# Masked queries on GpSimd and a later output projection in the second attention of a language-model tower

## The chip, the cores and the metric

The kernel runs on one NeuronCore of a Trainium2 chip as a single program. The metric is the device time of one execution in microseconds (us); lower is better. Within the core five engines run their own instruction streams and meet only at semaphores: TensorE (PE, matrix products into the eight PSUM banks; PEld is its weight load), VectorE (DVE), ScalarE (ACT), GpSimd (POOL) and SyncE (SP, transfers).

## The reference, cut to what matters

A tower of layers works on 16 sequences of 128 tokens: a token model (embedding, memory, four MLP layers, head), a fast-weight attention, a mixture of experts, then a second attention, then a second mixture of experts. The part that the change touches is the second attention (64 channels, 8 heads of 8):

```python
qk = (x @ Wqk.T).reshape(Bb, Nn, 2, Hh, hd)
patch_score = softmax(einsum('bhnd,bhmd->bhnm', q, k) * scale)
pos_score = softmax((rel @ Wpos.T + bpos).transpose(2, 0, 1))
g = sigmoid(gating)[None, :, None, None]
attn = (1.0 - g) * patch_score + g * pos_score[None]
attn = attn / attn.sum(axis=-1, keepdims=True)
out = einsum('bhnm,bhmd->bhnd', attn, v).transpose(0, 2, 1, 3).reshape(Bb, Nn, Cc)
return out @ Wproj.T + bproj
```

It is fed with the layer norm of the residual stream h, and its result is added to h; the last mixture of experts normalises that sum again.

## The kernel before, in words

All data is float32. The 16 sequences are the tiles t = 0 to 15 of 128 tokens each, and four of them make a chunk c (CH = 4, NC = 4). The residual stream stays in SBUF as H. Every engine's order is written out by hand: each block of the program is a list of calls to small helpers, and what an engine waits for is written as semaphore waits.

The second attention is a loop over the 16 tiles ("step t", j = t mod 4) on TensorE, ScalarE and VectorE, each with its own loop body. One step does, per engine:

- TensorE: scores(t+1) (8 products into banks 2 and 3, L1768 and L1769), on every odd step values_back (L1805, into bank 7), values(t-1) (L1792, bank 6), and turn_scores(t) (eight transposes of the exponentiated scores into banks 4 and 5, L1780). Once per chunk, spread over its four steps, it also does work for the next chunk: turn_input (L1815, bank 0) at j = 0, project_qk (L1824 and L1825: queries to bank 1, keys to bank 0) at j = 1, project_v (L1830, bank 1) at j = 3. positional (L1839, bank 1) comes at steps 4 and 12. At steps 7, 11 and 15 it turns the attended tiles of the chunk before (turn_attended, L1849, bank 0) and after turn_scores multiplies them with the output weights (project_out, L1855, bank 0).
- VectorE: normalise(t): for each of the two score banks a maximum (L2493) and a subtraction into SBUF (L2497). scores(t+1) can only start when this is done, since there is one pair of score banks; normalise(t+1) can only start when scores(t+1) is done. Then come, per chunk, the work around the norms: mix (reciprocal of the sums, gate, two more operations, L2507 to L2514, at j = 2; two of the four read two tensors of SBUF, L2509 and L2514), add_attended (L2520, adds project_out's bank to H) with e_stats (L409, L412) at j = 0, and e_apply (four TENSOR_SCALAR of L424) at j = 1.
- ScalarE: take_turned(t-1) (L1225, two copies of banks 4 and 5 to SBUF), the exponential of step t (L1242), save_values_T (L1217) on even steps, and per chunk: take_x (L1184), queries (L1189), take_keys (L1194), take_values (L1198), take_attended (L1203), take_positions (L1209).

The heads are separated by masks. A chunk's queries are copied four times out of bank 1, each time scaled by another column of the mask m4 (one scale per partition), into the four planes of qd[c % 2]: queries(c, h0, h1), L1189. For chunks 1 to 3 two of the four copies are made at step 4(c-1)+1 and two at the step after it. The first scores of a chunk wait for all four (semaphore d_qd), and so does project_v, since it overwrites bank 1.

GpSimd has little to do here: the norms' reciprocal roots (rstd_twice, L400 and L402) and some adds.

## Time and profile before

| | |
|---|---|
| median of 3 runs | 621.32 us |
| runs | 621.87, 620.23, 621.32 us |
| the profiled execution | 620.74 us |
| its span, first to last instruction | 619.0 us |
| mean granted TensorE clock | 0.984 |
| busy: PE, DVE, ACT, POOL | 545.0, 427.1, 358.0, 347.0 us |
| second attention (scores of tile 0 to the last turn_scores) | about 478 to 553 us |

Starts are microseconds from the span's first instruction. The profiled execution's own time is 1.7 us more than its span and 0.6 us below the median. In the timeline a row is one instruction, or several equal ones in a row merged (xN); a bracket at its end is the idle time of its engine just before it and what ended it.

### The profile page before, as it was taken

Reading aid. Unit: us, or ns where it says so; the run is one execution under the profiler, and the core shown is the slowest. Engines: PE = TensorE matmul, PEld = TensorE weight load, DVE = VectorE, ACT = ScalarE, POOL = GpSimd, SP = SyncE. Lnnn points to the kernel's source line nnn. Section 1 sums busy time; section 2 is a strip of 40 time slices with the busy share of each in tenths; the row PEclk is TensorE's granted clock in tenths of the full one; section 3 lists DMA queues with packets and bytes.
Section 4 is the critical chain, followed back from the end, with each engine's and each line's share of the span. In section 5 each row is a group of like instructions: output and inputs, shape, how many; then the busy total and the mean of one; then the engine's idle time right before and its main releaser. Section 6 shows DMA issues by size and latency. Waiting matters only on the chain.

```text
span 619.0 us, 12438 instructions
## 1 busy us (share of the span) xinstructions
PE 545.0 (88%) x4494; PEld 414.5 (67%) x4494; DVE 427.1 (69%) x1088; ACT 358.0 (58%) x949; POOL 347.0 (56%) x474
## 2 busy tenths in 40 slices
PE   7989999999987867779788888998999698889996
PEld 3556767778434656558677777886578576765785
DVE  4943563423887868798989988899526987756444
ACT  1264444444676765224768878874696666757430
POOL 2597653311360767798889899998267310001445
PEclk9999999999999999987999999999999999989999
DMA  8000000000000434300000000000000000000000
GB/s 278 17 1 1 2 0 1 1 1 1 1 2 1 75 71 77 81 0 2 2 1 1 1 2 2 0 2 1 2 2 2 1 2 1 2 2 1 9 9 18
DMA packets 10860, 10.43 MB, mean 17 GB/s; under 512 B 6000, under 2 KB 9840, under 8 KB 10544
## 3 DMA queue, kind: packets, MB, share of 16 engines
q1 hardware_dynamic: 8080, 7.54, 4.5%
q0 software_dynamic: 2144, 1.75, 1.5%
q8 instruction: 36, 0.59, 0.4%
q10 hardware_dynamic: 576, 0.35, 0.2%
q14 instruction: 24, 0.20, 0.1%
HBM read 5.77 MB, written 0.52 MB: 10 GB/s over the span
## 4 chain that ended last, share of the span: by engine, by line
PE 52%; DVE 21%; POOL 9%; ACT 7%; issue 5%; DMA 4%; SPq 2%; DVEq 0%; POOLq 0%; ACTq 0%
PE bank L1354 8%; PE bank L1342 7%; PE bank L1441 7%; PE bank L1657 5%; PE bank L1723 5%; DVE bank L2173 3%; PE bank L1615 3%; DVE features L2167 2%; DMA coefs<-weights 2%; PE bank L1720 2%; PE bank L1432 2%; POOL features L600 2%; PE bank L1768 2%; DVE features L2143 2%; SPq L460 2%
## 5 line engine op out<-in xcount | busy, mean ns | idle before, releaser
L1441 PE MATMUL bank<-ident,features 128*128 128x128 f32 x604 | 79.0, 280 | 10.4 <-DVE features L2143 7.1
L1441 PEld LDWEIGHTS bank<-ident,features 128*128 128x128 f32 x604 | 69.0, 145 | 19.0 <-DVE features L2143 13.8
L909 ACT ACTIVATE G<-bank,cols 128x512 f32<-128x512 f32 x64 | 43.9, 687 | 52.9 <-PE bank L1342 52.9
L600 POOL TENSOR_TENSOR features<-UV,coefs 128x1024 f32<-128x1024 f32 (+3 forms) x36 | 59.8, 1684 | 4.0 <-DVE UV L2130 4.0
L1354 PE MATMUL bank<-weights,G 128*128 128x128 f32 x512 | 59.9, 275 | 0.0
L1342 PE MATMUL bank<-xs,weights 128*128 128x512 f32 x128 | 57.8, 594 | 0.9 <-ACT xs L900 0.9
L1354 PEld LDWEIGHTS bank<-weights,G 128*128 128x128 f32 x512 | 58.5, 192 | 0.0
L2143 DVE TENSOR_TENSOR features<-UV,bank 128x1024 f32<-128x1024 f32 (+3 forms) x68 | 55.6, 861 | 0.7 <-ACT bank L992 0.2
L400 POOL TENSOR_SCALAR rstd<-mv 128x4 f32<-128x4 f32 x8 | 1.6, 195 | 92.7 <-DVE mv L412 92.7
L999 ACT ACTIVATE xs<-UV,coefs 128x32 f32<-128x32 f32 x232 | 50.4, 308 | 0.0
L999 ACT ACTIVATE sx<-UV,coefs 128x32 f32<-128x32 f32 x200 | 43.5, 307 | 0.0
L573 POOL TENSOR_TENSOR UV<-xs,rows 128x512 f32<-128x512 f32 x16 | 20.2, 1270 | 38.7 <-DVE xs L2032 38.6
L1432 PE MATMUL bank<-features 32*128 32x136 f32 x768 | 32.4, 299 | 10.4 <-issue 2.8
L2173 DVE TENSOR_REDUCE bank<-features 128x32 f32<-128x1024 f32 (+3 forms) x40 | 41.0, 1050 | 0.0
L1342 PEld LDWEIGHTS bank<-xs,weights 128*128 128x128 f32 x128 | 23.1, 190 | 25.0 <-issue 22.7
L1615 PE MATMUL bank<-RK,ident 128*128 128x256 f32 x160 | 38.3, 388 | 0.0
L424 DVE TENSOR_SCALAR UV<-xs,mv,rstd 128x128 f32<-128x128 f32 x52 | 20.8, 462 | 24.9 <-POOL rstd L393 23.2
L1432 PEld LDWEIGHTS bank<-features 32*128 32x128 f32 x768 | 27.0, 193 | 15.9 <-issue 5.5
L393 POOL TENSOR_TENSOR rstd<-rstd,neghalf 128x4 f32<-128x4 f32 x32 | 33.4, 1045 | 2.7
L2032 DVE TENSOR_TENSOR xs<-bank,UV 128x512 f32<-128x512 f32 x16 | 11.0, 690 | 33.2 <-PE bank L1354 31.2
L2167 DVE TENSOR_TENSOR features<-RK,bank 128x1024 f32<-128x1024 f32 (+3 forms) x32 | 32.2, 1007 | 0.8
L1615 PEld LDWEIGHTS bank<-RK,ident 128*128 128x128 f32 x160 | 29.7, 194 | 3.5
(362 smaller groups left out, 1348.0 us busy)
## 6 DMA issues: line engine op xcount, KB each, us to landing
weights<-in_w SPq DMA_DIRECT2D x2, 1024.0 KB, 10.2
features<-in_tok SPq DMA_DIRECT2D x1, 768.0 KB, 5.8
weights<-in_ew SPq DMA_DIRECT2D x4, 128.0 KB, 3.1
weights<-in_ew SPq DMA_DIRECT2D x2, 256.0 KB, 2.9
coefs<-G POOLq DMA_DIRECT2D x16, 25.5 KB, 4.7
rows<-in_rows SPq DMA_DIRECT2D x1, 384.0 KB, 6.4
out_h<-H SPq DMA_DIRECT2D x3, 128.0 KB, 2.0
coefs<-G SPq DMA_DIRECT2D x14, 25.5 KB, 5.1
```

Source lines behind the costliest of these rows:

```text
L393: pool.tensor_tensor(rstd[:, k, 0:n], rstd[:, k, 0:n], neghalf[:, 0:n], ALU.pow).then_inc(s["ln_rstd"], 1)
L600: pool.tensor_tensor(out, u, co, ALU.mult).then_inc(s["held_p"], 1)
L909: act.activation(G[:, 4 * (w % 2) + f, :], up_bank(f)[:], ACT.Gelu, bias=col("b1", 4 * i + f)).then_inc(s["tok_gelu"], 1)
L999: last = act.activation(own[t % 2][:, k, DH * h:DH * h + DH], UV[:, FIRST[t] + k, 0, DH * h:DH * h + DH], ACT.Copy, scale=C[:, t, 2 * NH + ...
L1342: mm(up_bank(f)[:], w1[:, i, P * f:P * f + P], xT[:, w % 2, :], start=True, stop=True).then_inc(s["tok_up"], 1)
L1354: last = mm(down_bank(w)[:, DT * j:DT * j + DT], G[:, 4 * (w % 2) + f, P * j:P * j + P], w2[:, i, f, :], start=(f == 0), stop=(f == 3))
L1432: last = mm(bank[4 * k + j][:, GB * SL * n:GB * SL * n + GB * SL], feat[left + k][x, g, 0:T].rearrange("p s b -> p (s b)"), feat[right + k ...
L1441: last = mm(out[:, P * k:P * k + P], x[:, P * k:P * k + P], ident[:], is_transpose=True, start=first and k == 0, stop=last_ and k == n - 1 ...
L1615: mm(bank[1][:, HB:2 * HB], ident[:], RK[:, 0, :], start=True, stop=True)
L2143: dve.tensor_tensor(out, u, co.unsqueeze(3).broadcast_to([P, R, NH, DH]), ALU.mult)\
L2167: ch(dve.tensor_tensor(PD[:, j, 0:R * HB].rearrange("p (r x) -> p r x", r=R), RK[:, r0:r1_, :], e.unsqueeze(1).broadcast_to([P, R, HB]), A ...
L2173: ch(dve.tensor_reduce(bankCR[:, r0:r1_, :], PD[:, j, 0:(r1_ - r0) * HB].rearrange("p (r h j) -> p r h j", r=r1_ - r0, h=NH), AX_X, ALU.add))
```

## The change

Six things differ.

1. ScalarE makes no masked queries for chunks 2 and 3. At step 5 and step 9 it makes one plain copy of bank 1 into a free buffer of SBUF (take_queries, target qraw), in the place of two scaled copies; the two of steps 6 and 10 go. Chunks 0 and 1 stay as they were.
2. GpSimd makes these four planes from qraw with four TENSOR_SCALAR multiplications of 128x512 per chunk, chunk 2 before and chunk 3 after the root of the norm of chunk 0's result.
3. project_v of chunks 2 and 3 waits for the plain copy alone; the first scores of chunks 2 and 3 wait for GpSimd (d_qpool).
4. project_out of chunks 0 and 1 moves on TensorE from the end of steps 7 and 11 to the end of steps 8 and 12, and writes bank 1, not bank 0. For that bank it also waits for take_values of chunk c+2 and, for chunk 1, for take_positions. turn_input(3) no longer waits for the addition but for take_attended(0); project_qk(3) now waits for the addition.
5. On VectorE add_attended and e_stats move from steps 8 and 12 to steps 9 and 13; e_apply moves from steps 9 and 13 to step 11 and step 14 (there behind mix).
6. Two semaphores are merged into others (utab_mm into u_mm, mean_mm into router_mm) with the counts of the later waits raised by one. Nothing is added or taken from the instructions there.

```diff
+        qraw = FT[:, 8704:9216]
...
+        def out_bank(c):
+
+            return bank[1 if c < 2 else 0]
...
             rstd_pool(pool, ch, ("d", NC - 1), CH)
             second_norm(NC - 1)
-            for c in range(NC):
+            def queries(c):
+
+                pool.wait_ge(s["q_raw"], c - 1)
+                for h in range(NH // 2):
+                    pool.tensor_scalar(qd[c % 2][:, h, :], qraw, m4[:, h:h + 1], None, ALU.mult).then_inc(s["d_qpool"], 1)
+
+            queries(2)
+            rstd_twice(pool, ch, ("e", 0), CH)
+            queries(3)
+            for c in range(1, NC):
                 rstd_twice(pool, ch, ("e", c), CH)
...
+            def take_queries(c):
+
+                act.wait_ge(s["d_q"], c + 1)
+                if c == 3:
+                    act.wait_ge(s["d_qpool"], NH // 2)
+                act.activation(qraw, bank[1][:], ACT.Copy).then_inc(s["q_raw"], 1)
...
                     elif j == 1:
-                        queries(c + 1, 0, 2)
+                        if c:
+                            take_queries(c + 1)
+                        else:
+                            queries(1, 0, 2)
                         take_keys(c + 1)
                     elif j == 2:
-                        queries(c + 1, 2, NH // 2)
+                        if not c:
+                            queries(1, 2, NH // 2)
...
                 if t % CH == 0:
-                    pe.wait_ge(s["d_qd"], NH // 2 * (t // CH + 1))
+                    if t < 2 * CH:
+                        pe.wait_ge(s["d_qd"], NH // 2 * (t // CH + 1))
+                    else:
+                        pe.wait_ge(s["d_qpool"], NH // 2 * (t // CH - 1))
...
             def project_out(c):
                 pe.wait_ge(s["at_xT"], c + 1)
+                if c < 2:
+                    pe.wait_ge(s["d_vcopy"], c + 3)
+                if c == 1:
+                    pe.wait_ge(s["pos_saved"], 2)
                 for j in range(CH):
-                    last = mm(bank[0][:, D * j:D * j + D], xa[:, 1, P * j:P * j + P], wproj[:], start=True, stop=True)
+                    last = mm(out_bank(c)[:, D * j:D * j + D], xa[:, 1, P * j:P * j + P], wproj[:], start=True, stop=True)
...
-                if j == 3 and c:
-                    project_out(c - 1)
+                if t == T - 1 or j == 0 and c >= 2:
+                    project_out(NC - 2 if j else c - 2)
...
-                if j == 0 and c >= 2:
+                if j == 1 and c >= 2:
                     add_attended(c - 2)
                     e_stats(c - 2)
-                if j == 1 and c >= 2:
-                    e_apply(c - 2)
                 if j == 2 and c:
                     mix(c - 1)
+                if t in (11, 14):
+                    e_apply(c - 2)
```

TensorE at the end of step 7, before (L1849 turn_attended(0), L1830 project_v(2), L1780 turn_scores(7), L1855 project_out(0), L1768 the first product of scores(9)):

```order
L1849 MATMUL bank0<-ident,RK 64x128 [waits d_kcopy,comb_done]
L1830 MATMUL bank1<-weights,sx 128x64 [waits d_qd]
L1780 MATMUL bank4<-ident,features 128x128 [waits p_ready,s_exp]
L1780 MATMUL bank5<-ident,features 128x128 [waits p_ready]
L1855 MATMUL bank0<-weights,sx 128x64 [waits at_xT]
L1768 MATMUL bank2<-features 128x128 [waits s_sub]
```

The same place now, and on to the first product of scores(10) (new lines: L1882 turn_attended, L1863 project_v, L1808 turn_scores, L1796 scores, L1820 values, L1843 turn_input, L1892 project_out; rows in between are the rest of the same groups):

```order
L1882 MATMUL bank0<-ident,RK 64x128 [waits d_kcopy,comb_done]
L1863 MATMUL bank1<-weights,sx 128x64 [waits q_raw]
L1808 MATMUL bank4<-ident,features 128x128 [waits p_ready,s_exp]
L1796 MATMUL bank2<-features 128x128 [waits s_sub]
L1820 MATMUL bank6<-UV,coefs 32x128 [waits p_ready]
L1843 MATMUL bank0<-ident,UV 128x128 [waits at_xT,d_kcopy,d_norm]
L1892 MATMUL bank1<-weights,sx 128x64 [waits d_vcopy,at_xT]
L1796 MATMUL bank2<-features 128x128 [waits s_sub]
```

project_out(0) now stands behind turn_scores(8), one pair of scores later, and writes bank 1.

VectorE in steps 13 and 14, before (L424 e_apply(1), L2493 and L2497 normalise(14), L2507 to L2514 mix(2)):

```order
L424 TENSOR_SCALAR xs<-H,mv,rstd 128x128 [waits ln_rstd,ln_var]
L424 TENSOR_SCALAR xs<-H,mv,rstd 128x128 x3
L2493 TENSOR_REDUCE RK<-bank2 128x4 [waits s_mm0]
L2497 TENSOR_TENSOR features<-bank2,RK 128x512 [waits dve_chain,s_T]
L2493 TENSOR_REDUCE RK<-bank3 128x4 [waits s_mm1]
L2497 TENSOR_TENSOR features<-bank3,RK 128x512 [waits dve_chain]
L2507 RECIPROCAL comb<-bank7 128x32 [waits at_T,pos_saved,av_back]
L2509 TENSOR_TENSOR comb<-comb,gate 128x32 [waits dve_chain]
L2512 TENSOR_TENSOR RK<-bank7,comb 128x256 [waits dve_chain]
L2514 TENSOR_TENSOR RK<-RK 128x256 [waits dve_chain]
L2493 TENSOR_REDUCE RK<-bank2 128x4 [waits s_mm0]
```

The same place now, from the end of normalise(14) to the start of normalise(15) (L429 is e_apply(1), L2544 to L2551 mix(2)):

```order
L2544 RECIPROCAL comb<-bank7 128x32 [waits at_T,pos_saved,av_back]
L2546 TENSOR_TENSOR comb<-comb,gate 128x32 [waits dve_chain]
L2549 TENSOR_TENSOR RK<-bank7,comb 128x256 [waits dve_chain]
L2551 TENSOR_TENSOR RK<-RK 128x256 [waits dve_chain]
L429 TENSOR_SCALAR xs<-H,mv,rstd 128x128 [waits ln_rstd,ln_var]
L429 TENSOR_SCALAR xs<-H,mv,rstd 128x128 x3
L2530 TENSOR_REDUCE RK<-bank2 128x4 [waits s_mm0]
```

e_apply(1) has moved from ahead of normalise(14) to between mix(2) and normalise(15); in its old place stand the addition and e_stats of chunk 1.

GpSimd behind the last add of the norms (L843), now (L879 the queries, L405 and L407 the root of chunk 0's norm):

```order
L843 TENSOR_TENSOR H<-H,rows 128x256 [waits d_norm]
L879 TENSOR_SCALAR features<-features,m4 128x512 [waits q_raw]
L879 TENSOR_SCALAR features<-features,m4 128x512 x3
L405 TENSOR_SCALAR rstd<-mv 128x4 [waits ln_var]
L407 TENSOR_TENSOR rstd<-rstd,neghalf 128x4 [waits pool_chain]
L879 TENSOR_SCALAR coefs<-features,m4 128x512 [waits q_raw]
L879 TENSOR_SCALAR coefs<-features,m4 128x512 x3
```

Before, the roots followed directly on the add.

## Rows read from the trace of the kernel before

**Rows 1.** The page: shares of the chain that ended last, by engine.

```profile
PE 52%; DVE 21%; POOL 9%; ACT 7%; issue 5%; DMA 4%; SPq 2%; DVEq 0%; POOLq 0%; ACTq 0%
```

**Rows 2.** Timeline of DVE, steps 6 to 10: start us, us, what [idle before].

```profile
509.49 0.69 DVE L2493 TENSOR_REDUCE RK<-bank 128x4 f32<-128x512 f32 x1
...
511.61 0.69 DVE L2497 TENSOR_TENSOR features<-bank,RK 128x512 f32<-128x512 f32 x1
513.94 0.69 DVE L2493 TENSOR_REDUCE RK<-bank 128x4 f32<-128x512 f32 x1 [1.64 <-PE bank L1768]
...
518.22 0.42 DVE L2520 TENSOR_TENSOR H<-bank,H 128x256 f32<-128x256 f32 x1 [1.48 <-PE bank L1855]
...
519.62 0.66 DVE L2493 TENSOR_REDUCE RK<-bank 128x4 f32<-128x512 f32 x1
...
523.64 0.69 DVE L2493 TENSOR_REDUCE RK<-bank 128x4 f32<-128x512 f32 x1 [0.23 <-PE bank L1768]
```

**Rows 3.** Timeline of PE, from scores(8) to scores(9), and turn_scores(8).

```profile
512.74 0.37 PE L1768 MATMUL bank<-features 64*128 64x128 f32 x1 [0.55 <-ACT features L1189]
...
516.30 1.04 PE L1780 MATMUL bank<-ident,features 128*128 128x128 f32 x8
517.18 1.00 PE L1855 MATMUL bank<-weights,sx 128*128 128x64 f32 x8
518.12 0.37 PE L1768 MATMUL bank<-features 64*128 64x128 f32 x1
...
520.27 1.04 PE L1780 MATMUL bank<-ident,features 128*128 128x128 f32 x8
```

**Rows 4.** Timeline of ACT, step 5: the first two masked queries of chunk 2.

```profile
507.37 1.27 ACT L1189 ACTIVATE features<-bank,m 128x512 f32<-128x512 f32 x2 [1.62 <-PE bank L1824]
```

**Rows 5.** Timeline of PE: the first products of scores(12), scores(13) and scores(14).

```profile
531.23 0.37 PE L1768 MATMUL bank<-coefs 64*128 64x128 f32 x1 [0.55 <-ACT coefs L1189]
...
536.60 0.37 PE L1768 MATMUL bank<-coefs 64*128 64x128 f32 x1
...
541.08 0.37 PE L1768 MATMUL bank<-coefs 64*128 64x128 f32 x1
```

**Rows 6.** Timeline of DVE: starts of normalise(13), e_apply(1), normalise(14), normalise(15).

```profile
538.11 0.66 DVE L2493 TENSOR_REDUCE RK<-bank 128x4 f32<-128x512 f32 x1
...
540.80 1.11 DVE L424 TENSOR_SCALAR xs<-H,mv,rstd 128x128 f32<-128x128 f32 x4
542.27 0.69 DVE L2493 TENSOR_REDUCE RK<-bank 128x4 f32<-128x512 f32 x1 [0.36 <-PE bank L1768]
...
546.40 0.69 DVE L2493 TENSOR_REDUCE RK<-bank 128x4 f32<-128x512 f32 x1
```

**Rows 7.** Timelines of ACT and of PE at step 15, the attention's end.

```profile
549.87 0.59 ACT L1203 ACTIVATE sx<-bank 64x512 f32<-64x512 f32 x1 [1.29 <-PE bank L1849]
550.36 1.04 ACT L1242 ACTIVATE features<-features 128x1024 f32<-128x1024 f32 x1
...
551.46 1.57 PE L1780 MATMUL bank<-ident,features 128*128 128x128 f32 x8 [1.63 <-ACT features L1242]
```

**Rows 8.** Stretches: us, busy (x) of PE, PEld, DVE, ACT, POOL, then PEclk, DMA, GB/s.

```profile
551.50:555.50 4.00, 4.00 (x22) 4.00 (x23) 0.80 (x4) 1.20 (x2) 0.00 (x0) 0.57 0.00 0
```

**Rows 9.** GpSimd operations of 128x512, grouped by form: xcount | busy us, mean ns.

```profile
L800 POOL COPY xs<-sx 128x512 f32<-128x512 f32 x2 | 1.2, 610 | 0.1
L573 POOL TENSOR_TENSOR UV<-xs,rows 128x512 f32<-128x512 f32 x16 | 20.2, 1270 | 38.7 <-DVE xs L2032 38.6
L450 POOL TENSOR_TENSOR coefs<-coefs 128x512 f32<-128x512 f32 x1 | 1.5, 1514 | 0.1
```

**Rows 10.** Timelines of DVE and POOL: L2380 without and with GpSimd beside it.

```profile
564.19 0.68 DVE L2380 TENSOR_TENSOR coefs<-RK 128x512 f32<-128x512 f32 x1
584.21 0.94 DVE L2380 TENSOR_TENSOR coefs<-RK 128x512 f32<-128x512 f32 x1
...
584.68 0.78 POOL L880 TENSOR_TENSOR H<-H,features 128x128 f32<-128x128 f32 x1
```

More of the change, by code:

```diff
@@ L1295, in _ @@
             pe.wait_ge(s["load_tables"], 32)
-            mm(bank[0][0:VOC, 0:DT], embT[:], wupd[:], start=True, stop=True).then_inc(s["utab_mm"], 1)
+            mm(bank[0][0:VOC, 0:DT], embT[:], wupd[:], start=True, stop=True).then_inc(s["u_mm"], 1)
             pe.wait_ge(s["tables_ready"], 1)
@@ L1623, in means @@
                 if c == NC - 1:
-                    last.then_inc(s["mean_mm"], 1)
+                    last.then_inc(s["router_mm"], 1)
             tr = nc.tensor.transpose
@@ L1812, in turn_input @@
                 if c >= 3:
-                    pe.wait_ge(s["d_add"], c - 2)
+                    pe.wait_ge(s["at_xT"], c - 2)
                 for j in range(CH):
@@ L1823, in project_qk @@
                     pe.wait_ge(s["pos_saved"], 1)
+                if c >= 3:
+                    pe.wait_ge(s["d_add"], c - 2)
                 mm(bank[1][:], wq, xa[0:D, 0, :], start=True, stop=True).then_inc(s["d_q"], 1)
@@ L1827, in project_v @@
             def project_v(c):
-                pe.wait_ge(s["d_qd"], NH // 2 * (c + 1))
+                if c < 2:
+                    pe.wait_ge(s["d_qd"], NH // 2 * (c + 1))
+                else:
+                    pe.wait_ge(s["q_raw"], c - 1)
                 for j in range(CH):
@@ L1978, in _ @@
             one_hot(1)
-            dve.wait_ge(s["utab_mm"], 1)
+            dve.wait_ge(s["u_mm"], 1)
             dve.wait_ge(s["load_update"], 16)
@@ L1993, in memory @@
             def memory(c):
-                dve.wait_ge(s["u_mm"], c + 1)
+                dve.wait_ge(s["u_mm"], c + 2)
                 dve.tensor_tensor_scan(memT[:, 512 * c:512 * c + 512], keep[:, 512 * c:512 * c + 512],
@@ L2416, in _ @@
             CAPACITY = float(-(-N * 5 // (4 * E)))
-            dve.wait_ge(s["router_mm"], 1)
+            dve.wait_ge(s["router_mm"], 2)
             ch(tt(rout[0:T, 3, :], bank[7][0:T, 64:64 + E], row("br0", parts=T), plus))
@@ L2420, in _ @@
             small_softmax(rout[0:T, 3, :], 0, rout[0:T, 0, :]).then_inc(s["r_prob"], 1)
-            dve.wait_ge(s["router_mm"], 2)
+            dve.wait_ge(s["router_mm"], 3)
             sc = rout[0:T, 4, :]
```

13 lines of the change are left out of this document (7 added, 6 removed).

## The prediction

> **What bounds the kernel now.** I read the chain of waits first: TensorE and VectorE hold 73% of it [rows 1], and in the second attention they hand it to each other once per step, with two detours over ScalarE. So I read that stage in the timelines of the engines. scores(t+1) needs normalise(t) done; normalise(t+1) needs scores(t+1). From the first row of normalise(7) at 509.49 to the end of its last at 511.61 + 0.69 = 512.30 are 2.80 us, and from the first product of scores(8) to normalise(8) are 513.94 - 512.74 = 1.20 us [rows 2, 3]. That makes 4.0 us a step if nothing else is in the way; normalise(9) to normalise(10) has it, 523.64 - 519.62 = 4.02 [rows 2]. Two steps are far above it: normalise(8) to normalise(9) takes 519.62 - 513.94 = 5.68, and its twin, a chunk later, ends at 538.11 [rows 2, 6]. In both TensorE is the late one, and project_out is the last thing in its queue ahead of the scores: it starts at 517.18, the scores at 518.12 [rows 3], while normalise(8) was over at 516.74 (513.94 + 2.80). The reader should also see two waits on ScalarE: scores(8) and scores(12) each follow 0.55 us of idle TensorE, ended by the last masked query [rows 3, 5].
>
> **The change, part by part.** I follow the start of normalise(t) and call its shift against the profile d(t).
>
> Queries of chunk 2. normalise(7) ends at 512.30, so without the query wait scores(8) could start at 512.36 and not at 512.74: d(8) = -0.38 [rows 2, 3]. This needs GpSimd done by 512.3. The plain copy can start where the first masked one did, 507.37 [rows 4]; two masked ones took 1.27 together, so one copy takes about 0.6 and GpSimd starts at 508.05. It has 4.3 us for four operations, **1.07 us each**. The trace shows no multiplication of this kind on GpSimd. Nearest rows of 128x512: a copy 0.61 us, a product of two tensors 1.27 and once 1.51 [rows 9]. The new operation reads one tensor, as the copy does, and computes, as the product does; I take 0.8, nearer to the copy, and keep 0.61 and 1.51 as ends. At 0.8 it is done at 511.3 and hidden. For chunk 3 the same working gives a start of about 525.05 and scores(12) at 529.45, 4.4 us, 1.1 each.
>
> The Trainium skill, "GPSIMD Engine Reference", section "Performance versus the Vector engine", gives about 1.8 cycles per element as the best for a tight one-operation loop and says that elementwise work belongs on VectorE; an estimate from it is 0.77 us for 512 elements, which would leave the sum as it is. No run here shows it yet.
>
> project_out(0) out of step 7. From scores(8) to project_out are 517.18 - 512.74 = 4.44 us of TensorE work (values_back, values, turn_attended, project_v, turn_scores) [rows 3]. scores(9) now stands in its place: about 512.36 + 4.44 + 0.1 = 516.9 (the 0.1 because a group of scores behind transposes starts that much later), and normalise(9) 1.2 later, at 518.1, with no addition ahead of it: d(9) = 518.1 - 519.62 = -1.5.
>
> project_out(0) into step 8. From scores(9) to turn_scores(8) are 520.27 - 518.12 = 2.15 us, and eight transposes hold the queue for 517.18 - 516.30 = 0.88: 3.0 us, and 4.0 with the projection's 0.94 (518.12 - 517.18) [rows 3], so scores(10) can start at 516.9 + 4.0 = 520.9. normalise(9) ends at 518.1 + 2.8 = 520.9: the projection fits. Behind it VectorE now does the addition and e_stats, 519.62 - 518.22 = 1.40 us [rows 2], 521.0 to 522.4, where scores(10) is done at 522.1: d(10) = 522.4 - 523.64 = -1.2. Step 10 goes on as before with mix(1) as its limit, d(11) about -1.35.
>
> Step 11. Without the query wait scores(12) starts at the end of normalise(11), 529.45, against 531.23 [rows 5]; e_apply(0), 1.11 us [rows 6], is over at 530.4, before scores(12) is: d(12) = -1.8. TensorE's queue to scores(13) was 536.60 - 531.23 = 5.37 [rows 5], now 0.94 less: scores(13) at 533.9, normalise(13) at 535.1, **d(13) = -3.0**.
>
> Then most of the second half is paid back. Step 12 holds positional, and its queue was already full: 541.08 - 536.60 = 4.48 [rows 5]. With project_out(1) it is 5.4, so scores(14) starts at 539.3. VectorE waits for that projection for its addition, and with e_stats (1.40) normalise(14) begins at 540.75: d(14) = -1.5. Behind normalise(14) now stand mix(2) (1.4, from the end of the four rows to 546.40, rows 6) and e_apply(1), which was hidden in step 13: 540.75 + 2.7 + 1.4 + 1.1 = 546.0, against 546.40. d(15) is only -0.4.
>
> The end. normalise(15) ends at 546.0 + 2.8 = 548.8, but what counts is the exponential of step 15, which started at 550.36, not at VectorE's end (549.20): take_attended(2) at 549.87 stood ahead of it in ScalarE's queue [rows 7]. That path follows scores(15), which needs normalise(14). From the start of normalise(14) to that exponential were 550.36 - 542.27 = 8.1 us [rows 6, 7], so it comes at 540.75 + 8.1 = 548.85. Both meet there: **-1.5 us** at the last turn_scores. Behind it the same program runs with TensorE busy to the end, so the shift is passed on whole. ScalarE's saved copies count no further: it idles in every step.
>
> GpSimd against VectorE. The new operations run from 508.05 and 525.05, just when mix(0) (it lies right ahead of 509.49, rows 2) and mix(1) stand on VectorE ahead of a normalise that waits for them. L2380, which reads two tensors of SBUF, took 0.68 us alone and 0.94 with a GpSimd operation beside it, itself 0.78 long [rows 10]. mix has two operations with two SBUF inputs. I take 0.2 us for each mix, 0.4 in sum; bounds 0 and 4 x 0.26 = 1.0. Both delays pass on, since TensorE's queue follows.
>
> The semaphore merges raise counts that are passed in the same order: nothing, or below what can be measured. Sum: -1.5 + 0.4 = **-1.1 us**, 620.74 - 1.1 = 619.6 for a profiled execution and 621.32 - 1.1 = **620.2** for the median (the profiled one lay 0.6 below it).
>
> **The rivals.** A measurement of this kernel tells about 0.3% (1.9 us) from no change.
>
> A: the forecast, -1.1, from -1.9 to 0 with the bounds of the contention and of the GpSimd price up to 1.27. Chance 0.58.
>
> B: GpSimd locks VectorE out. If each two-input operation of mix waits for a whole GpSimd operation, half of 0.8 on average and at worst all of it, four of them cost 1.6 to 3.2 instead of 0.4: +0.1 to +1.7, time about 621.6. For it: the 0.26 of rows 10. Against: that is a third of the GpSimd operation, not the whole. The Trainium skill, "SBUF — State Buffer", section "Who interferes with whom", says that the shared port pair is an exclusive lock held for the whole instruction, and that a VectorE instruction with two SBUF inputs contends with a GpSimd one that reads SBUF. By that rule the case is this rival; rows 10 agree in direction, not in size. Chance 0.12.
>
> C: slower, by GpSimd's price. Above 1.07 us every 0.1 costs 0.4 at scores(8) and, above 1.1, as much at scores(12). At 1.27 it is 0.8 + 0.7 = 1.5: the gain is gone. From there on the kernel is slower; at 1.51 [rows 9] it is (1.51 - 1.07) x 4 + (1.51 - 1.10) x 4 = 3.4, less 1.5: +1.9, 623.2. For it: one row of a simple product had 1.51. Against: that one reads two tensors. Chance 0.10.
>
> D: more than forecast, by the clock. At the attention's end TensorE idled 1.63 us before turn_scores(15) [rows 7], and in the 4 us after it the granted clock is 0.57, at its lower level of 1.2 GHz for most of them: 4 x 0.43 = 1.7 us lost [rows 8]. In my schedule both ends of that idle time move by 1.5 us (the one follows scores(15), the other VectorE), so it stays about as long and I expect the fall to stay. If it went, the change would give -2.8, 618.5. Chance 0.20, in which smaller slips of mine in step 13 to 15, where the 3.0 us of d(13) shrink to 1.5, are counted too.
>
> **How the numbers follow.** 620.2 is the likeliest. The range runs from 618.5 (D) to 622.6 (B at its worst with half of the 0.6 by which medians stray here); what lies outside is the dear end of C and a deeper fall of the clock, under 0.2. Faster by over 0.3% (below 619.5): D and the edge of A, 0.25. Slower by over 0.3% (above 623.2): the dear part of C, with 0.04 for a longer low clock, 0.10. The rest, 0.65, is within.
>
> **What the profile of the changed kernel would show.** GpSimd's multiplications at about 0.8 us, the last of four done before the idle time of scores(8) ends; scores(8) and scores(12) released by normalise, not by queries. normalise(8) to normalise(9) near 4.5 us instead of 5.68. A gap on VectorE ahead of the addition of chunk 1, and over 5 us from normalise(14) to normalise(15), with mix and e_apply in it. The last turn_scores about 1 us earlier. The forecast is wrong if a multiplication takes over 1.1 us, if mix grows by more than 0.5 us, or if the stretch at the lower clock behind step 15 changes its length.

## The result

| | median us | runs | lowest to highest |
|---|---|---|---|
| kernel before | 619.70 | 8 | 617.82 to 621.87 |
| changed kernel | 625.64 | 8 | 624.18 to 628.74 |

The ratio is 1.010, with a 95% interval of 1.0071 to 1.013: the change makes the kernel slower, by 5.9 us between the medians. The forecast was 1.1 us faster, and its range ended at 622.6. The profiled execution of the changed kernel took 624.18 us, with a span of 622.3 (before: 620.74 and 619.0). Here and below medians are over all executions of a kernel, while ratios leave out the few that took over 1.5% longer than the kernel's fastest (the traces of e1 and e2 are of such executions).

GpSimd's timeline is the first thing to read: start us, us, what, xcount, idle time before and its releaser. The four masked queries of chunk 2 and of chunk 3, and one operation by itself:

```profile
507.45 6.21 POOL L879 TENSOR_SCALAR features<-features,m 128x512 f32<-128x512 f32 x4 [3.28 <-ACT features L1211]
509.01 1.57 POOL L879 TENSOR_SCALAR features<-features,m 128x512 f32<-128x512 f32 x1
527.91 6.31 POOL L879 TENSOR_SCALAR coefs<-features,m 128x512 f32<-128x512 f32 x4 [1.21 <-ACT features L1211]
```

One operation takes 1.56 to 1.58 us by itself and 1.55 in a row of four, not 0.8 (one of the eight, which runs beside VectorE's e_apply, takes 1.68). Its source came when the prediction said: all of this trace lies 0.63 us earlier, from stages that the change doesn't touch, and 507.45 + 0.63 = 508.08, where the prediction had 508.05. So the four end at 513.66, which is 514.29 on the prediction's time axis, where it had 511.3: 3.0 us later. TensorE's timeline shows who waits for that (L1808 turn_scores, L1796 scores, L1833 values_back, L1820 values, L1892 project_out):

```profile
509.81 1.09 PE L1808 MATMUL bank<-ident,features 128*128 128x128 f32 x8 [0.30 <-ACT features L1263]
513.71 0.37 PE L1796 MATMUL bank<-features 64*128 64x128 f32 x1 [2.81 <-POOL features L879]
...
515.21 1.11 PE L1833 MATMUL bank<-picked,UV 128*128 128x128 f32 x4
516.25 1.08 PE L1820 MATMUL bank<-UV,coefs 128*32 128x128 f32 x16
...
518.77 1.04 PE L1808 MATMUL bank<-ident,features 128*128 128x128 f32 x8
519.75 0.37 PE L1796 MATMUL bank<-features 64*128 64x128 f32 x1
...
520.84 0.64 PE L1820 MATMUL bank<-UV,coefs 128*32 128x128 f32 x16
...
522.78 1.00 PE L1892 MATMUL bank<-weights,sx 128*128 128x64 f32 x8
523.80 0.37 PE L1796 MATMUL bank<-features 64*128 64x128 f32 x1
```

Where [rows 3] had 0.55 us of idle time ahead of scores(8), there are 2.81 now, ended by GpSimd. A second thing stands in these rows: the 16 instructions of values take 1.08 us right after the wait and 0.64 a step later. The granted clock tells why. TensorE alone, in four stretches of the changed kernel: us, busy (x), PEclk, DMA share, GB/s.

```profile
510.00:515.00 5.00, 2.19 (x24) 0.93 0.00 0
515.00:516.00 1.00, 1.00 (x8) 0.50 0.00 0
515.00:520.00 5.00, 5.00 (x48) 0.73 0.01 3
535.00:540.00 5.00, 5.00 (x49) 0.68 0.00 0
```

From about 0.6 us behind each of the two waits, TensorE is granted 0.50, its lower level of 1.2 GHz, for some 3 us, though it is then busy without a gap. Before the change the clock was 1.00 in all these steps.

VectorE's timeline of the changed kernel has the counterpart of [rows 2] and [rows 6] (L2530 opens a normalise, L2546 and L2551 are the operations of mix with two SBUF inputs, L2557 the addition, L429 e_apply):

```profile
507.64 0.54 DVE L2546 TENSOR_TENSOR comb<-comb,gate 128x32 f32<-128x32 f32 x1
...
508.67 0.42 DVE L2551 TENSOR_TENSOR RK<-RK 128x256 f32<-128x256 f32 x1
...
515.30 0.69 DVE L2530 TENSOR_REDUCE RK<-bank 128x4 f32<-128x512 f32 x1 [3.48 <-PE bank L1796]
...
520.94 0.69 DVE L2530 TENSOR_REDUCE RK<-bank 128x4 f32<-128x512 f32 x1 [2.83 <-PE bank L1796]
...
528.29 0.35 DVE L2546 TENSOR_TENSOR comb<-comb,gate 128x32 f32<-128x32 f32 x1
...
532.20 1.48 DVE L429 TENSOR_SCALAR xs<-H,mv,rstd 128x128 f32<-128x128 f32 x4
...
545.86 0.42 DVE L2557 TENSOR_TENSOR H<-bank,H 128x256 f32<-128x256 f32 x1 [1.55 <-PE bank L1892]
...
551.36 1.11 DVE L429 TENSOR_SCALAR xs<-H,mv,rstd 128x128 f32<-128x128 f32 x4
```

From such rows I took the start of every normalise and lined up the steps of all kernels at normalise(0). This table carries most of what follows. A column gives the us from one normalise to the next, the last row the whole stage from normalise(0) to the exponential of step 15. "Forecast" is the prediction's schedule written in the same way, without its 0.4 for contention. The last three columns are experiments told of below.

| step | before | forecast | changed | e1 | e3 | e12 |
|---|---|---|---|---|---|---|
| 0 to 7 | 30.06 | 30.06 | 30.21 | 30.07 | 30.88 | 30.23 |
| 7 to 8 | 4.45 | 4.07 | **6.29** | 4.44 | 4.10 | 5.88 |
| 8 to 9 | 5.68 | 4.56 | **5.64** | 4.53 | 4.57 | 4.54 |
| 9 to 10 | 4.02 | 4.32 | 4.28 | 4.28 | 4.27 | 4.27 |
| 10 to 11 | 4.33 | 4.18 | 4.26 | 4.11 | 4.92 | 4.26 |
| 11 to 12 | 4.45 | 4.00 | **6.46** | 4.45 | 4.11 | 5.99 |
| 12 to 13 | 5.69 | 4.49 | **5.56** | 4.52 | 4.56 | 4.53 |
| 13 to 14 | 4.16 | 5.66 | 5.76 | 5.77 | 5.76 | 5.76 |
| 14 to 15 | 4.13 | 5.23 | 5.13 | 5.12 | 5.12 | 5.13 |
| 15 to exponential | 3.96 | 2.86 | 2.93 | 2.93 | 2.94 | 2.93 |
| stage | 70.93 | 69.43 | 76.52 | 70.22 | 71.23 | 73.52 |

The changed kernel's stage is 5.59 us longer than before, and the medians differ by 5.9. Against the forecast four steps are off, two per wait for GpSimd; the other steps agree to 0.15 us.

At the attention's end the fall of the clock [rows 8] isn't in this trace, although TensorE idles for the same time before turn_scores(15). The first row is TensorE's timeline of the changed kernel:

```profile
556.41 1.09 PE L1808 MATMUL bank<-ident,features 128*128 128x128 f32 x8 [1.63 <-ACT features L1263]
```

The second is the stretch behind it:

```profile
556.40:560.40 4.00, 3.99 (x43) 1.00 0.00 0
```

### The profile page after: what moved, and what is told of

Same layout as the page of the kernel before. It is cut to its first block, busy times and chain, and to the rows that moved or that the text cites. A ratio compares the mean times of both kernels' runs of the same rounds, so it can differ in the third digit from the quotient of the medians.

```text
span 622.3 us, 12444 instructions
## 1 busy us (share of the span) xinstructions
PE 544.4 (87%) x4494; PEld 413.9 (67%) x4494; DVE 427.9 (69%) x1088; ACT 354.8 (57%) x943; POOL 359.7 (58%) x482
## 3 DMA queue, kind: packets, MB, share of 16 engines
HBM read 5.77 MB, written 0.52 MB: 10 GB/s over the span
## 4 chain that ended last, share of the span: by engine, by line
PE 33%; DVE 15%; POOL 7%; ACT 4%; issue 2%; DVEq 0%; POOLq 0%
PE bank L1466 6%; PE bank L1682 5%; PE bank L1748 5%; DVE bank L2210 3%; PE bank L1640 2%; DVE features L2204 2%; PE bank L1745 2%; PE bank L1796 2%; POOL features L605 2%; DVE features L2180 2%; PE bank L1820 1%; PE bank L1808 1%; POOL features L625 1%; POOL coefs L879 1%; DVE features L2534 1%
## 5 line engine op out<-in xcount | busy, mean ns | idle before, releaser
L1466 PE MATMUL bank<-ident,features 128*128 128x128 f32 x604 | 76.1, 275 | 11.3 <-DVE features L2180 8.2
L1466 PEld LDWEIGHTS bank<-ident,features 128*128 128x128 f32 x604 | 66.8, 142 | 18.8 <-DVE features L2180 14.1
L405 POOL TENSOR_SCALAR rstd<-mv 128x4 f32<-128x4 f32 x8 | 1.6, 195 | 79.5 <-DVE mv L417 79.5
L1457 PE MATMUL bank<-features 32*128 32x136 f32 x768 | 34.0, 307 | 11.6 <-issue 4.2
L1457 PEld LDWEIGHTS bank<-features 32*128 32x128 f32 x768 | 28.4, 199 | 17.2 <-issue 7.6
L429 DVE TENSOR_SCALAR UV<-xs,mv,rstd 128x128 f32<-128x128 f32 x52 | 20.8, 463 | 24.9 <-POOL rstd L398 23.2
```

Source lines behind the costliest of these rows:

```text
L1457: last = mm(bank[4 * k + j][:, GB * SL * n:GB * SL * n + GB * SL], feat[left + k][x, g, 0:T].rearrange("p s b -> p (s b)"), feat[right + k ...
L1466: last = mm(out[:, P * k:P * k + P], x[:, P * k:P * k + P], ident[:], is_transpose=True, start=first and k == 0, stop=last_ and k == n - 1 ...
```

## The experiments

The theory after the first reading: (1) a GpSimd multiplication costs 1.55 us, which makes scores(8) and scores(12) wait; (2) that idle time brings the clock down, which costs as much again; (3) the moved projection works as forecast. Rivals: the moved projection itself delays a step and the query wait only fills what it leaves; the slow steps 8 to 9 and 12 to 13 come from contention or from bank 1; GpSimd holds VectorE up. In the diffs, a line with + is the experiment's. Each ratio is to the kernel before, timed beside the experiment; a time without a ratio is of one execution.

### One part alone: e1 and e2

e1 keeps the moved projection, and ScalarE makes all masked queries as before (the waits that belong to them are as before too).

```diff
-            queries(2)
-            rstd_twice(pool, ch, ("e", 0), CH)
-            queries(3)
-            for c in range(1, NC):
+            for c in range(NC):
...
-                        if c:
-                            take_queries(c + 1)
-                        else:
-                            queries(1, 0, 2)
+                        queries(c + 1, 0, 2)
```

> The changed kernel with ScalarE making all masked queries again, as in the kernel before; the later output projection, its bank and the moved norm steps stay. Theory (the loss is GpSimd's: its masked multiplication took 1.55 us instead of the forecast 0.8, so scores(8) and scores(12) wait for it, and TensorE's clock falls in those waits): without it 1.1 to 1.5 us below the kernel before, no fall of the clock behind scores(8) and scores(12), normalise(8) to normalise(9) near 4.5 us. Rival (the moved projection and norm steps cost by themselves, in steps 12 to 14): at or above the kernel before, by 1 us or more.

e2 keeps GpSimd's queries and puts project_out (with its bank and its waits), the addition, e_stats and e_apply back to where they were.

```diff
-                if t == T - 1 or j == 0 and c >= 2:
-                    project_out(NC - 2 if j else c - 2)
+                if j == 3 and c:
+                    project_out(c - 1)
```

> The kernel before with the masked queries of chunks 2 and 3 on GpSimd and nothing else of the change. Theory (GpSimd's price): the start of scores(8) 1.4 to 1.9 us later than before and that of scores(12) 3 to 4, plus about 1 us for each fall of the clock behind them: 4 to 7 us above the kernel before, like the changed kernel or above it. Rival (the moved projection is what costs): within 1.5 us of the kernel before.

e1: 619.25 us, ratio 0.9973 (0.9943 to 1.0003), stage 70.22. e2: 629.2 us, ratio 1.0128 (1.0093 to 1.0163), stage 78.25. So the queries alone cost more than the whole change, somewhat above the 4 to 7 us expected, and the projection alone is worth 0.7 us in the stage (1.1 to 1.5 were expected; as a time it is 1.7, with an interval that just reaches the kernel before). The parts don't simply add: 7.3 - 0.7 = 6.6, and the whole change has 5.6. The missing 1.0 us lies between normalise(11) and normalise(13): 14.16 us in e2 against 10.14 before, 12.02 in the changed kernel against 8.97 in e1. There e2's clock is low for over 6 us, twice as long as in the changed kernel; what sets that length isn't shown. VectorE's timeline of e1 shows the prediction's d(9) as forecast, 525.66 - 521.13 = 4.53, and so its twin, 543.02 - 538.50 = 4.52, with the gap ahead of the addition of chunk 1 (L2544):

```profile
521.13 0.69 DVE L2517 TENSOR_REDUCE RK<-bank 128x4 f32<-128x512 f32 x1 [1.63 <-PE bank L1786]
...
525.66 0.69 DVE L2517 TENSOR_REDUCE RK<-bank 128x4 f32<-128x512 f32 x1 [1.72 <-PE bank L1786]
...
533.01 0.19 DVE L2533 TENSOR_TENSOR comb<-comb,gate 128x32 f32<-128x32 f32 x1
...
538.50 0.69 DVE L2517 TENSOR_REDUCE RK<-bank 128x4 f32<-128x512 f32 x1 [0.61 <-PE bank L1786]
...
543.02 0.69 DVE L2517 TENSOR_REDUCE RK<-bank 128x4 f32<-128x512 f32 x1 [1.72 <-PE bank L1786]
...
547.39 0.42 DVE L2544 TENSOR_TENSOR H<-bank,H 128x256 f32<-128x256 f32 x1 [1.55 <-PE bank L1879]
```

The rivals that blame the projection or bank 1 fall with that. In e2 TensorE's clock falls in the same two places:

```profile
515.00:520.00 5.00, 3.71 (x36) 0.66 0.00 0
...
537.00:543.00 6.00, 5.12 (x42) 0.50 0.00 0
```

### The price of GpSimd's operation: e3 and e4

e3 makes the same planes with a TENSOR_TENSOR, the mask's column repeated along the row as the second input.

```diff
-                    pool.tensor_scalar(qd[c % 2][:, h, :], qraw, m4[:, h:h + 1], None, ALU.mult).then_inc(s["d_qpool"], 1)
+                    pool.tensor_tensor(qd[c % 2][:, h, :], qraw, m4[:, h:h + 1].broadcast_to([P, CH * P]), ALU.mult)\
+                        .then_inc(s["d_qpool"], 1)
```

> The changed kernel with GpSimd multiplying by the mask column as a second tensor read over and over (step 0) in a tensor-tensor product, not as a scalar per partition. Theory (only the duration of this operation decides): it takes 1.04 to 1.27 us as the other products of 128x512 do; then scores(8) is late by at most 0.8 us against 2.0 now, and the total is 3 to 6 us below the changed kernel, between -1.5 and +1 against the kernel before. Rival (any GpSimd work in that place delays VectorE and TensorE, whatever it takes): 2 us or less below the changed kernel.

e4 leaves the masks of chunks 2 and 3 out and copies qraw four times.

```diff
-                    pool.tensor_scalar(qd[c % 2][:, h, :], qraw, m4[:, h:h + 1], None, ALU.mult).then_inc(s["d_qpool"], 1)
+                    pool.tensor_copy(qd[c % 2][:, h, :], qraw).then_inc(s["d_qpool"], 1)
```

> The changed kernel with GpSimd copying the raw queries into the four planes instead of multiplying them with the mask; the masks of chunks 2 and 3 are left out, so this part of the output is not computed as the reference does. Theory (the duration of one GpSimd operation is the cause): at the copy's 0.61 us the four are done in 2.5, scores(8) and scores(12) are released by VectorE or TensorE, the clock stays up behind them, and the stage from normalise(0) to the last exponential is 69.5 to 70.0 us, against 70.9 before and 76.5 in the changed kernel. Rival (a GpSimd beside VectorE is enough of a cost): mix(0) and mix(1) stretched so far that the stage stays above 70.9.

e3: 621.52 us, ratio 1.0021 (0.9991 to 1.0052), stage 71.23. e4: 620.66 us in a single execution, stage 70.53, above the 69.5 to 70.0 that was expected. GpSimd's timeline of e3, the four of chunk 2 and two by themselves:

```profile
508.80 4.21 POOL L879 TENSOR_TENSOR features<-features,m 128x512 f32<-128x512 f32 x4 [3.25 <-ACT features L1212]
508.80 1.04 POOL L879 TENSOR_TENSOR features<-features,m 128x512 f32<-128x512 f32 x1 [3.25 <-ACT features L1212]
509.80 1.04 POOL L879 TENSOR_TENSOR features<-features,m 128x512 f32<-128x512 f32 x1
```

The product takes 1.04 us where the same work as TENSOR_SCALAR takes 1.57, and the copy of e4 takes 0.61. At 1.04 both waits are gone: 7 to 8 takes 4.10, 11 to 12 takes 4.11, no clock falls, and 8 to 9 and 12 to 13 are 4.57 and 4.56. Every step is then as forecast but those that hold a mix: 0 to 7 is 0.82 longer than before, 10 to 11 is 0.74 longer than forecast. VectorE's timeline of e3 at mix(0):

```profile
509.02 0.87 DVE L2547 TENSOR_TENSOR comb<-comb,gate 128x32 f32<-128x32 f32 x1
509.92 0.42 DVE L2550 TENSOR_TENSOR RK<-bank,comb 128x256 f32<-128x256 f32 x1
510.38 0.74 DVE L2552 TENSOR_TENSOR RK<-RK 128x256 f32<-128x256 f32 x1
```

L2550, with one input in PSUM, keeps its length. L2547 takes 0.87 where e1 has 0.19 at the same place of mix(1), and it ends at 509.89, 0.05 after the GpSimd operation that ran at its start (508.80 + 1.04 = 509.84). L2552 takes 0.74, not 0.42, and ends at 511.12, 0.28 after the one that ran at its start (509.80 + 1.04 = 510.84). At mix(1) it is the same, 0.68 and 0.74. In e4, with copies of 0.61 beside them, the two take 0.43 and 0.85 at mix(0) and 0.24 and 0.85 at mix(1). In all eight cases the shorter operation ends 0.04 or 0.05 us, the longer one 0.28 or 0.29 us after the end of the GpSimd operation that had begun last before it. So the wait is that for the rest of a GpSimd operation, as rival B had it: 1.56 us in e3 for both mixes together. That is a reading of eight operations in two kernels.

The Trainium skill, "SBUF — State Buffer", section "Who interferes with whom", has the shared port pair as an exclusive lock for the whole instruction; these rows agree with that rule. Those with GpSimd's TENSOR_SCALAR don't, which reads one tensor and one scalar per partition: in the changed kernel L2546 (507.64 + 0.54) ends at 508.18, in the middle of a GpSimd operation that runs from 507.45 to 509.03, and L2551 keeps its 0.42. There the wait has another end: L2546 ends 0.73 us after the start of the GpSimd operation at mix(0), and 0.73 after it at mix(1) (528.64 against 527.91), though it began at 0.19 in the one and at 0.38 in the other. The same operation in e2, e5, e5b and e12 has 0.72 to 0.74; that makes ten cases in five kernels. So GpSimd's TENSOR_SCALAR held it up for the first part of its 1.57 us only; why is open.

### The clock in the two waits: e5, e5b and e12

These keep the changed kernel whole and give TensorE dummy products while it waits for GpSimd. They write a part of bank 1 that nobody reads any more.

```diff
+                if t in (2 * CH, 3 * CH):
+                    pe.wait_ge(s["q_raw"], t // CH - 1)
+                    for k in range(26):
+                        mm(bank[1][:, 256:384], ident[:], ident[:], start=True, stop=True)
```

> The changed kernel with 26 products of the identity with itself (128x128, result unused, into bank 1) on TensorE ahead of scores(8) and of scores(12), so that the engine works through most of the wait for GpSimd. Theory that the fall of the clock in these waits is a part of the loss: granted clock 1.0 behind both, normalise(8) to normalise(9) about 4.5 us instead of 5.64, and 2.0 to 2.5 us below the changed kernel in the stage. Rival (the long steps 8 and 12 come from the order of the work, not from the clock): no change from the changed kernel.

26 products were too many: they last longer than the wait, and normalise(7) to normalise(8) takes 8.82 us, 2.5 more than in the changed kernel. The time is 626.53 (ratio 1.0109, 1.0063 to 1.0155), so as a time it settles nothing, and the 2.0 to 2.5 us that the stage was to gain are missed. The step behind the wait does settle it: 4.53 us and not 5.64, in an otherwise equal program. So e5b has 12 of them, and e12 is the same kernel as e5b, timed ten times.

```diff
-                    for k in range(26):
+                    for k in range(12):
```

> As the filler experiment before, with 12 products instead of 26: those took 5.5 us and kept scores(8) waiting themselves, 12 take about 2.6 and end before GpSimd does. Theory (each fall of the clock costs 1.1 us): normalise(8) at the same place as in the changed kernel (36.5 us after normalise(0)), then 4.5 us to normalise(9) instead of 5.64, and a stage of 74.3 us instead of 76.5. Rival: the stage stays at 76.5.

> The changed kernel with 12 dummy products of 128x128 in each of the two waits for GpSimd (the kernel of e5b again, now timed in rounds): TensorE is kept at work through part of the wait, nothing is spared. One execution of e5b had 618.66 with a stage of 73.52 us against 76.52 in the changed kernel. If the fall of the clock in the two waits is what that difference is, it holds here: about 3 us below the changed kernel, ratio to before 1.005 or less. If e5b's one time was chance, the ratio is that of the changed kernel, 1.010.

e5b: 618.66 in a single execution, stage 73.52. e12: 623.36 us, ratio 1.004 (1.0009 to 1.0071), stage 73.52 again. Both stages are 0.8 below the 74.3 that was expected, since the scores right behind the wait run at the full clock too. The single 618.66 was a lucky one as a time, but the stage was not: e12's profiled execution took 626.64 with the same stage, and from 222 to 306 us, in stages that no experiment touches, the granted clock was 0.96 in e5b's and 0.88 in e12's. TensorE's timeline of e12, the wait for GpSimd filled and the scores behind it:

```profile
516.21 2.84 PE L1790 MATMUL bank<-ident 128*128 128x128 f32 x24
519.18 0.37 PE L1800 MATMUL bank<-features 64*128 64x128 f32 x1
...
520.27 0.66 PE L1837 MATMUL bank<-picked,UV 128*128 128x128 f32 x4
520.86 0.64 PE L1824 MATMUL bank<-UV,coefs 128*32 128x128 f32 x16
```

And TensorE alone in two stretches of e12 that hold both waits and what follows:

```profile
517.00:522.00 5.00, 4.87 (x61) 1.00 0.01 3
537.00:542.00 5.00, 4.78 (x60) 1.00 0.01 3
```

scores(8) still waits for GpSimd's fourth multiplication (512.92 + 6.20 = 519.12 in e12), and nothing else is spared; the work only keeps the clock at its higher level of 2.4 GHz. That is worth (6.29 - 5.88) + (5.64 - 4.54) = 1.5 us at chunk 2 and (6.46 - 5.99) + (5.56 - 4.53) = 1.5 us at chunk 3: **3.0 us of the changed kernel's loss are clock**, shown by adding work. As times the two kernels differ by 1.010 - 1.004 = 0.006 of 620, 3.7 us. Nor is the fall there a matter of one trace: it stands behind all four waits for GpSimd that TensorE spent idle (2.78 to 2.90 us, in the changed kernel and e2) and behind none of the six that were filled (e5, e5b, e12).

### Further with the projection: e7 and e9

With the queries on ScalarE, their wait can be shortened in place. e7 is e1 with the second two masked queries of chunks 2 and 3 behind the exponential of steps 6 and 10, and e_apply(1) at step 15, behind normalise(15).

```diff
+                if j == 2 and 0 < c < 3:
+                    queries(c + 1, 2, NH // 2)
                 if t and t % 2 == 0:
                     save_values_T(t // 2 - 1)
...
-                if t in (11, 14):
+                if t in (11, 15):
                     e_apply(c - 2)
```

> The later projection without GpSimd's queries, with two more edits: at steps 6 and 10 ScalarE makes the last two masked queries ahead of save_values_T, not behind it, and VectorE does e_apply of chunk 1 behind normalise(15), not ahead of it. If the two waits for the last query (0.55 us each) come only from that place in ScalarE's queue, and the payback in step 14 only from e_apply, the stage falls from 70.2 to 68.4 us, and the kernel lies 2.5 us below the one before (4 with the fall of the clock at the attention's end gone). If ScalarE's or TensorE's queue is the limit there, 69.5 or more.

e9 is e7 with project_out(1) at step 13 and its addition and e_stats at step 15; the wait of turn_attended for the addition stays for the last chunk alone.

```diff
-                if t == T - 1 or j == 0 and c >= 2:
-                    project_out(NC - 2 if j else c - 2)
+                if t in (8, 13, 15):
+                    project_out((8, 13, 15).index(t))
...
-                if j == 1 and c >= 2:
+                if t in (9, 15):
                     add_attended(c - 2)
                     e_stats(c - 2)
```

> As the kernel with the two edits, and the projection of chunk 1 one step later still, at step 13, where TensorE has no positional work; its addition and norm come behind normalise(15). If the full queue of step 12 is what pays the gain back, as the prediction said, normalise(13) to normalise(14) falls from 5.8 us to about 4.6 and the stage to 67.2 us. If not, the time comes back in step 13 or at the last exponential, and the stage stays at that of the kernel it starts from.

e7: 617.5 us, ratio 0.9942 (0.9911 to 0.9973), stage 69.65, where 68.4 was expected. e9: 616.24 us, ratio 0.9949 (0.9916 to 0.9982), stage 68.44, where 67.2 was expected. Both are faster than both kernels; which of the two is the faster isn't shown by their times, whose intervals overlap. The two query waits are gone (7 to 8 and 11 to 12 take 4.12), and normalise(13) to normalise(14) falls to 4.47 in e9, as expected, but both stages miss by the same 1.2 us. In e7 normalise(15) starts 65.69 us after normalise(0), the exponential 3.96 after that, and normalise itself lasts only 2.8. ScalarE's timeline of e9 shows what stands between them (L1221 take_attended(2), L1260 the exponential):

```profile
546.00 1.09 ACT L1243 ACTIVATE UV<-bank 128x512 f32<-128x512 f32 x2
548.37 0.59 ACT L1221 ACTIVATE sx<-bank 64x512 f32<-64x512 f32 x1 [1.29 <-PE bank L1872]
548.87 1.04 ACT L1260 ACTIVATE features<-features 128x1024 f32<-128x1024 f32 x1
```

It is the second of the two paths that the prediction saw meet at 548.85. I had forgotten it when VectorE's got shorter. The next experiments test that.

### The end of the attention: e10, e11 and e13

e10 is e9, and e11 is the kernel before, each with take_attended(2) behind the exponential of step 15.

```diff
-                if t == T - 1:
-                    take_attended(NC - 2)
                 act.wait_ge(s["s_sub"], 2 * t + 2)
...
-                if j == 3 and c and t < T - 1:
+                if j == 3 and c:
                     take_attended(c - 1)
```

> e9 with one edit: ScalarE makes the copy of the attended channels of chunk 2 behind the exponential of step 15, not ahead of it. In e9 that exponential started 4.02 us after the start of normalise(15); normalise(15) itself lasts 2.8. If ScalarE's order is what held it, it now starts about 2.9 after normalise(15), 67.3 us after normalise(0) (e9: 68.44), and TensorE idles some 0.5 us before the last turn_scores and not 1.63: 1.1 us less, 615.1 where e9 has 616.2. If the clock fall that e9's profile shows behind that idle time hangs on its length, it is gone here. Rival: the transposes of step 15 are held by something else on TensorE (values(14), turn_attended); then the time of e9 stays, within 0.3 us.

> The kernel before with the same single edit. VectorE ended normalise(15) at 549.20 there and the exponential started at 550.36, so it can start 1.1 us earlier: the stage from normalise(0) to the exponential of step 15 takes 69.8 us, not 70.93, and TensorE's idle time before the last turn_scores is 0.5 us. If the fall of the clock to 0.57 behind it goes with the idle time, another 1.7 us: 2.8 in all, ratio 0.9955. If the fall comes whatever that idle time is: 1.1, ratio 0.998.

e10: 615.22 us, ratio 0.9927 (0.9895 to 0.9959), stage 67.59. e11: 618.67 us, ratio 0.997 (0.9945 to 0.9995), stage 69.81 where 69.8 was expected; both ratios that were expected, 0.9955 and 0.998, lie inside that interval, so the time doesn't choose between them. ScalarE's timeline of e10:

```profile
542.97 1.08 ACT L1243 ACTIVATE UV<-bank 128x512 f32<-128x512 f32 x2
544.66 1.06 ACT L1258 ACTIVATE features<-features 128x1024 f32<-128x1024 f32 x1 [0.60 <-DVE features L2522]
545.62 0.58 ACT L1221 ACTIVATE sx<-bank 64x512 f32<-64x512 f32 x1
```

The exponential now follows VectorE, 2.84 us after normalise(15). The stage is 67.59 and not 67.3, since 0 to 7 took 0.33 longer than in e9, ahead of the edit. TensorE's idle time before turn_scores(15) is 0.46 us in e10 and 0.52 in e11. e10 has the shortest stage and the lowest median of this study; as a time its interval overlaps those of e7 and e9.

Left was the fall of the clock behind that idle time, 1.7 us in the first trace of before. e13 is the kernel before, unchanged, profiled again.

> The kernel before, unchanged, profiled once more. Its first trace has 1.63 us of idle TensorE before the last turn_scores and a granted clock of 0.57 in the 4 us behind it; the changed kernel has the same 1.63 us and 1.00. If the fall follows from the kernel's own sequence, it is there again, at the same place and of the same length (about 1.7 us lost). If it differs from execution to execution, the same idle time stands in this trace with a clock of 1.00 behind it; then the 1.7 us of the first comparison of traces were chance. The stage from normalise(0) to the exponential of step 15 is 70.93 us either way.

It took 617.64 us with a stage of 71.13 (0.20 more than in the first trace, all of it in 0 to 7), and the same 1.63 us of idle TensorE is there. Its timeline:

```profile
549.99 1.09 PE L1780 MATMUL bank<-ident,features 128*128 128x128 f32 x8 [1.63 <-ACT features L1242]
```

The stretch behind it, which answers to [rows 8]:

```profile
549.99:553.99 4.00, 4.00 (x43) 1.00 0.00 0
```

No fall. In e9 there was one behind the same idle time, in a profiled execution of 620.72 where the median is 616.24:

```profile
549.90:553.90 4.00, 3.94 (x19) 0.50 0.01 2
```

Twelve traces have these 1.63 us; three show the fall (before, e2, e9), nine don't, and one and the same kernel shows both. So at this place it belongs to an execution, not to a kernel. Its length differs too: some 3 us in the first trace of before, over 6 us in e2 and e9. What decides either stays open.

## Why the prediction was wrong

**The step that failed** is the price of GpSimd's multiplication: "The new operation reads one tensor, as the copy does, and computes, as the product does; I take 0.8, nearer to the copy, and keep 0.61 and 1.51 as ends." It measured 1.56 to 1.58, above the upper end. The inference was wrong in kind: the number of inputs read doesn't order these operations, since one tensor with a scalar per partition (1.57) is slower than the same tensor with the same column as a second input (1.04 in e3). One of the neighbours was also misread: L573 of [rows 9], 1.27, is an addition of a row repeated over the chunk's tiles and not a product, while the trace of before holds eleven products of 128x512 with one factor repeated along part of the row (L831) at 1.04. The estimate of 0.77 from the Trainium skill, "GPSIMD Engine Reference", section "Performance versus the Vector engine", is half of what this form took (1.57); that page calls its figure the best of a tight loop, and I let it stand beside my 0.8 as if it spoke for it.

**Rival C named the mechanism and the thresholds.** They held where they were tried: at 1.04 us (e3) both waits are gone, as its budgets of 1.07 and 1.1 say. Its formula at 1.55 gives (1.55 - 1.07) x 4 + (1.55 - 1.10) x 4 = 3.7 us, and e12, which has the price without the clock, shows (5.88 - 4.07) + (5.99 - 4.00) = 3.8. What failed was its chance, 0.10, and that it ended with the wait.

**A missing term: the clock in the wait.** The prediction looked at the granted clock at the attention's end only, and no term asked what an added idle time does to TensorE. It is 3.0 us by e12. With it the sum closes: 69.43 forecast for the stage, +3.8 price, +3.0 clock, and what is left, 76.52 - 76.23 = 0.3, is about what the two steps with a mix are longer (30.21 - 30.06 and 4.26 - 4.18).

**Contention** was forecast at 0.2 for each mix. In the changed kernel the two-input operations give 0.54 - 0.19 = 0.35 at mix(0), and 0.16 at mix(1): 0.5 against 0.4, right in size by luck, since it holds for this form of GpSimd operation alone. With the cheaper ones rival B is what happens, 1.56 us in e3, and it eats the forecast gain: with a product that fits both budgets the change measured as no change (e3, 1.0021). The prediction gave B 0.12 because 0.26 of 0.78 in [rows 10] looked like a third of the lock. That was read against the wrong operation: L880 began 0.47 us after L2380. What ran when L2380 began stands one row earlier on GpSimd's timeline of before:

```profile
583.69 0.92 POOL L877 TENSOR_TENSOR features<-features 128x128 f32<-128x128 f32 x1
```

It ended at 584.61 and L2380 at 585.15, 0.54 later. That is L2380's 0.68 alone less 0.14, just as the 0.05 and 0.28 of e3 are 0.19 and 0.42 less 0.14. So [rows 10] agreed with the lock in size too; a stretched row only shows how much of the other operation was left when it began.

**What was right.** The moved projection: steps 8 to 9 and 12 to 13 at 4.5 us (e1, e3), 9 to 10 at 4.28 for 4.32, the payback in steps 13 and 14 (5.77 and 5.12 for 5.66 and 5.23), and the two paths that meet at the exponential (2.93 for 2.86). For e1 alone the forecast without its two query terms gives 1.50 - 0.38 - 0.45 = 0.67 of gain in the stage, and 0.71 was measured. The semaphore merges cost nothing that these rows show.

**Two slips in the sums of the rivals** change nothing here. A's bounds don't follow from its terms: -1.5 with 0 to 1.0 of contention and up to 1.5 of price runs from -1.5 to +1.0. B's 621.6 is counted from the profiled 620.74, where the others start at the median 621.32; counted alike it is 622.2, at worst 623.0. The measured 625.64 lies beyond either.

**Rival D** came in by its sign: the fall at the attention's end is absent in the changed kernel's trace. But e13 shows that this is an execution's chance. It was no property of the kernel before that a change could take away, and the prediction should not have had a case for it.

How far can one trace carry a comparison? The stage in the trace against the medians:

| | stage less before's 70.93, us | ratio less 1, of 620 us |
|---|---|---|
| changed | +5.6 | +6.2 |
| e2 | +7.3 | +7.9 |
| e5 | +8.3 | +6.8 |
| e12 | +2.6 | +2.5 |
| e3 | +0.3 | +1.3 |
| e1 | -0.7 | -1.7 |
| e11 | -1.1 | -1.9 |
| e7 | -1.3 | -3.6 |
| e9 | -2.5 | -3.2 |
| e10 | -3.3 | -4.5 |

The order is almost the same, and most differ by about 1 us (e5 by 1.5), inside the intervals (about 1.9 us either side, 2.9 for e5). The faster ones gain somewhat more than the stage shows; e7's 2.3 us more I can't explain.

## What to carry to other kernels

Before work goes to another engine with a deadline, its price must come from that very form of the operation, and if no row has it, the forecast should be made at the dear end and ask what the miss does. An added wait on TensorE costs its length and what the granted clock loses behind it, here nearly as much again (3.0 us on 3.8). When one of two paths that meet is shortened, look up the other's order first: e10's single moved copy gave 1.2 us at the last exponential (4.02 to 2.84), which two earlier kernels had left.

## What was not expected of the hardware

- GpSimd on 128x512 float32: TENSOR_SCALAR with a scalar per partition 1.56 to 1.58 us, TENSOR_TENSOR product with a column repeated along the row 1.04, TENSOR_TENSOR addition of a row repeated over four tiles 1.27 [rows 9], copy 0.61.
- A VectorE operation with two SBUF inputs waited for the rest of the running GpSimd TENSOR_TENSOR or copy (0.19 became 0.87, 0.42 became 0.74), but not for all of a TENSOR_SCALAR: there it ended 0.72 to 0.74 us after that operation's start, ten times of ten. VectorE's e_apply beside that TENSOR_SCALAR took 1.48 for 1.11, and the GpSimd operation 1.68.
- 12 useless products in each of two waits made the changed kernel faster: by 2.3 us in the medians (625.64 to 623.36), 3.7 in the ratios (1.010 to 1.004) and 3.0 in the stage.
- The same kernel has a granted clock of 0.57 in one execution and 1.00 in another over the 4 us behind the same 1.63 us of idle TensorE.
